# Global attention with separate score and maxima rings: the weighting issued once per step, behind both pairs of scores

## The chip, the cores and the metric

The kernel runs on one core of a Trainium2 chip. The metric is the device time of one execution in microseconds (us). TensorE (PE in the profile) multiplies matrices into PSUM, VectorE (DVE) and ScalarE (ACT) read PSUM, GpSimd (POOL) does small work on SBUF, SyncE (SP) mostly issues DMAs.

## The reference

A causal global attention and a local attention network read the same normalised input, and the output joins them. Only the global attention is touched by the change:

```python
scores = jnp.einsum('bhqd,bhkd->bhqk', q, k) / jnp.sqrt(jnp.asarray(D, x.dtype))
...
scores = jnp.where(causal[None, None], scores, -jnp.inf)
weights = jax.nn.softmax(scores, axis=-1)
out = jnp.einsum('bhqk,bhkd->bhqd', weights, v)
```

There are 16 heads of 16 numbers each and 4096 tokens. After it come the output projection, two layers of windowed attention and MLP, and a gate.

## The kernel before, in words

`global_attention` works on groups of four heads (4 groups, g) and blocks of 512 queries (8 blocks, j), 32 blocks in all; groups 0 and 2 run j upwards, groups 1 and 3 downwards. A block has one **step** for each tile of 128 keys that its queries may see, 4(j+1) of them, so 576 steps in all. The last four steps of a block are **diagonal**: the keys lie in the block's own range, the operands shrink to 512, 384, 256 and 128 queries, and a mask is added by a further matmul. The other 448 steps are **full**: 112 in each group.

A step has, for each of its four heads, a score matmul (128 keys by up to 512 queries, L585; its mask L592), an exponential on ScalarE (L485) that writes `probs`, and a weighting matmul (L606) that adds values times probabilities into the one bank `ps_o`. Heads go in two pairs, so a step has two **half-steps** (`hp` 0 and 1). In this text S0 to S3 are the four score matmuls of a step, E0 to E3 its exponentials.

The scores of the heads go through three PSUM banks, `ps_s` (SR = 3), in turn: score number n waits until exponential number n - 3 has been read out. So S3 of a step waits for E0 of the same step, and S2 for E3 of the step before.

The subtraction of the maximum is inside the score matmul, as extra rows of `qst`, so the row maxima of a block must be known before it starts. They come from a second pass of score matmuls, the **maxima**: a unit is two matmuls of up to 512 keys (L557, for the block's own keys a mask, L561), which VectorE reduces in one instruction (L509). Units have two PSUM slots of their own, `ps_m` (MR = 2); unit n waits for the reduction of unit n - 2. `pace` writes out in which half-step each unit is issued: mostly one, in group 0 every fourth half-step two, and a block's last unit about six half-steps before the block starts. When the last unit of a block is reduced, VectorE and GpSimd prepare the maxima, TensorE **turns** them (L567), VectorE copies them (L522) and SP issues their loads into `qst`; the block's first score waits for these.

ScalarE also copies `ps_o` out at the end of a block (`take_sums`, L474), behind the four exponentials of the next block's first step, and issues the loads of a later group's keys and values during the eight steps behind each of two group starts (L401 to L403).

TensorE takes its instructions in the order in which the block at the end of `global_attention` issues them. `weigh(s, half)` issues four matmuls, one for each head, over half of the queries (256 of 512 in a full step); each is two MATMUL records in the trace, so a half is "x8". The order before, for steps s and s+1:

```text
weigh(s, 0)   score(s+1, 1)   unit(s)   weigh(s, 1)   score(s+2, 0)   unit(s)   weigh(s+1, 0) ...
```

Of the kernel before, what the change touches and what calls it, by code (L numbers as in the profile page):

```python
# [17 lines left out]
C = 512  # L18
# [7 lines left out]
GH = 4  # L26
# [6 lines left out]
VW = 32  # L33
# [290 lines left out]
def global_attention(nc, k_parts, q_parts, v_aug, o_raw, ident, ones, nulls, identb, mask_k, mask_q):  # L324
# [5 lines left out]
    with ExitStack() as ctx:  # L330
        def sb(name, shape, dt=F32):
            return ctx.enter_context(nc.sbuf_tensor(name, shape, dt))
# [4 lines left out]
        QR, MR, SR, PR = 8, 2, 3, 3  # L337
        kst = [sb(f"kst{i}", [P, PAIRS, S], F32R) for i in range(2)]
        qst = [sb(f"qst{i}", [P, PAIRS, C], F32R) for i in range(QR)]
        vst = [sb(f"vst{i}", [P, NT, GH * VW]) for i in range(2)]  # L340
        probs = sb("probs", [P, PR, GH, C])
# [12 lines left out]
        ps_o = ctx.enter_context(nc.psum_tensor("ps_o", [P, C], F32))  # L354
# [14 lines left out]
        exp_done = sem("g_exp_done")  # L369
        pv_done = sem("g_pv_done")  # L370
        o_done = sem("g_o_done")
# [7 lines left out]
        NSTEP = len(steps)  # L379
        last_step = {st[0]: s for s, st in enumerate(steps)}  # L380
# [8 lines left out]
        def q_slot(b):  # L389
            return b % QR  # L390

        def q_use(b):
            return b // QR + 1
# [3 lines left out]
        def load_k(eng, g, j):  # L397
            cols = slice(j * C, (j + 1) * C)
            kh = k_parts[g * GH:(g + 1) * GH, :, :, cols].rearrange("(p x) t d n -> x (t d) p n", x=2)
            for x in range(2):  # L400
                eng.dma_start(kst[g % 2][ROWS * x:ROWS * x + 2 * D, :, cols].bitcast(F32), kh[x]).then_inc(k_in[g % 2][j], 16)  # L401
                eng.dma_start(kst[g % 2][ROWS * x + 2 * D:ROWS * x + KQ, :, cols].bitcast(F32), kh[x, 0:D]).then_inc(k_in[g % 2][j], 16)
            eng.dma_start(vst[g % 2][:, j * TPC:(j + 1) * TPC, :], v_aug[g, :, j * TPC:(j + 1) * TPC, :]  # L403
                          ).then_inc(k_in[g % 2][j], 16)
# [62 lines left out]
        @block.scalar  # L467
        def _(act):
            def take_sums(b):

                act.wait_ge(pv_done, 2 * last_step[b] + 2)
                if b >= 2:
                    act.wait_ge(o_out[b % 2], 16 * (b // 2))
                act.activation(o_sb[:, b % 2, :], ps_o[:, :], ACT.Copy).then_inc(o_done, 1)  # L474

            queue = []
            for s, (b, g, j, i) in enumerate(steps):
                off = max(0, i - TPC * j) * P

                if s >= PR:  # L480
                    act.wait_ge(pv_done, 2 * (s - PR) + 2)
                for h in range(GH):
                    n = GH * s + h
                    act.wait_ge(scored, n + 1)
                    act.activation(probs[:, s % PR, h, off:C], sslots[n % SR][:, off:C], ACT.Exp, scale=float(D) ** -0.5  # L485
                                   ).then_inc(exp_done, 1)
                if i == 0 and b > 0:
                    take_sums(b - 1)
                    if b % NC == 0 and b // NC + 1 < G:
                        queue = [(b // NC + 1, jj) for jj in range(NC)]  # L490
                elif queue:
                    load_k(act, *queue.pop(0))
            take_sums(NB - 1)
# [30 lines left out]
        @block.tensor  # L524
        def _(pe):
            pe.wait_ge(const_in, 12 * 16)
            pe.wait_ge(o_zero, 1)
            seen_k = set()
            seen_q = set()

            def need_k(g, j):
                for jj in range(j + 1):
                    if (g, jj) not in seen_k:
                        seen_k.add((g, jj))
                        pe.wait_ge(k_in[g % 2][jj], 16 * 5 * (g // 2 + 1))

            def do(unit):
                b = unit[1]
                g, j = order[b]
                n = place[unit]  # L540
                slot = mslots[n % MR]
                if n >= MR:
                    old = stream[n - MR]
                    if old[0] == "max":
                        pe.wait_ge(max_read, max_at[old] + 1)
                    else:
                        pe.wait_ge(mrow_done, old[1] + 1)
                if unit[0] == "max":
                    _, _, a, hp, cc = unit
                    if b not in seen_q:  # L550
                        seen_q.add(b)
                        pe.wait_ge(q_in[q_slot(b)], 16 * 6 * q_use(b))
                    need_k(g, cc)
                    width = P * (a + 1) if cc == j else C
                    for x in range(2):
                        rows = slice(ROWS * x, ROWS * x + ROWS)
                        last = pe.matmul(slot[:, x, 0:width], qst[q_slot(b)][rows, hp, a * P:(a + 1) * P],  # L557
                                         kst[g % 2][rows, hp, cc * C:cc * C + width], start=True, stop=True)
                    if cc == j:
                        for x in range(2):  # L560
                            last = pe.matmul(slot[:, x, a * P:width], id_b[:, :], mq_sb[:, :], start=False, stop=True,  # L561
                                             skip_group_check=True)
                    last.then_inc(max_scored, 1)
                else:
                    pe.wait_ge(split_done, b + 1)
                    for a in range(TPC):
                        last = pe.matmul(slot[0:GH * NPART, 0, a * P:(a + 1) * P],  # L567
                                         msplit[:, b % 2, a * GH:(a + 1) * GH, :].rearrange("p h t -> p (h t)").bitcast(F32),
                                         id_f[:, :], start=True, stop=True)
                    last.then_inc(turned, 1)  # L570

            def score(s, hp):
                b, g, j, i = steps[s]
                off = max(0, i - TPC * j) * P
                if i == 0 and hp == 0:

                    pe.wait_ge(m_in[q_slot(b)], 16 * GH * q_use(b))
                    need_k(g, j)
                diagonal = i >= TPC * j
                for x in range(2):  # L580
                    n = GH * s + 2 * hp + x
                    if n >= SR:
                        pe.wait_ge(exp_done, n - SR + 1)
                    rows = slice(ROWS * x, ROWS * x + ROWS)
                    last = pe.matmul(sslots[n % SR][:, off:C], kst[g % 2][rows, hp, i * P:(i + 1) * P],  # L585
                                     qst[q_slot(b)][rows, hp, off:C], start=True, stop=True)
                    if not diagonal:
                        last.then_inc(scored, 1)
                if diagonal:
                    for x in range(2):  # L590
                        n = GH * s + 2 * hp + x
                        pe.matmul(sslots[n % SR][:, off:off + P], id_b[:, :], mk_sb[:, :], start=False, stop=True,  # L592
                                  skip_group_check=True).then_inc(scored, 1)

            def weigh(s, half):
                b, g, j, i = steps[s]
                off = max(0, i - TPC * j) * P
                if half == 0:
                    if i == 0 and b > 0:

                        pe.wait_ge(o_done, b)
                    pe.wait_ge(exp_done, GH * s + GH)
                mid = (off + C) // 2
                lo, hi = ((off, mid), (mid, C))[half]
                for h in range(GH):
                    last = pe.matmul(ps_o[32 * h:32 * h + VW, lo:hi], vst[g % 2][:, i, h * VW:(h + 1) * VW],  # L606
                                     probs[:, s % PR, h, lo:hi], start=(i == 0 and half == 0), stop=(s == last_step[b]),
                                     tile_position=(0, 32 * h), skip_group_check=True)
                last.then_inc(pv_done, 1)

            for unit in first:
                do(unit)
            score(0, 0)
            score(0, 1)
            for t, (_, todo) in enumerate(plan):
                s, hp = t // 2, t % 2
                if hp:
                    weigh(s, 0)
                elif s >= 1:
                    weigh(s - 1, 1)  # L620
                if s + 1 < NSTEP:
                    score(s + 1, hp)
                for unit in todo:
                    do(unit)
            weigh(NSTEP - 1, 1)


def project_out(nc, y_rows, o_raw, w_o, b_o, bcast):
# [1006 lines left out]
```

## Time and profile before

| | before |
|---|---|
| median of 3 runs | 4113.04 us (4109.99 to 4122.79) |
| the profiled execution | 4123.71 us, its span 4121.9 us |
| PE busy in the span | 3442.6 us (84%) |
| DVE busy | 2534.4 us (61%) |
| ACT busy | 1695.8 us (41%) |
| mean granted TensorE clock | 0.921 of full |

The busy shares are averages over stages with different limits. The score matmuls of global attention run from 345 to 2037 us of the span. Timeline rows merge neighbouring instructions of a line: "x8" is eight instructions, the duration runs from the start of the first to the modelled end of the last. Ends of matmuls overlap the next instruction, so the cost of one to TensorE is read from its start to the start of what follows.

### The profile page before, as it was taken

The numbers are of one execution on the slowest core, as the hardware profiler recorded it, in microseconds if no ns is written. First come the engines' busy times: TensorE is split into PE (matmuls) and PEld (weight loads), VectorE is DVE, ScalarE is ACT, GpSimd is POOL, SyncE is SP. The second block draws the span as 40 slices with busy tenths as digits, with TensorE's granted clock in tenths as the row PEclk, the third lists the DMA queues.
The fourth block names the chain that finished last, engine by engine and source line by source line (L and its number), as shares of the span: only waits on it lengthen the run. The fifth ranks groups of instructions, "written<-read, shape, count | busy, mean of one in ns | idle before, by whom it ended". The sixth has DMA issues, their size and how long they took to land. (4 is left out here: it accounts for less than half of the span.)

```text
span 4121.9 us, 77619 instructions
## 1 busy us (share of the span) xinstructions
PE 3442.6 (84%) x32558; PEld 2063.7 (50%) x32684; DVE 2534.4 (61%) x3408; ACT 1695.8 (41%) x3089; POOL 669.0 (16%) x464
## 2 busy tenths in 40 slices
PE   5837999999999999999754899997697799996795
PEld 2412333333444333333333677775576677775675
DVE  4325887888777887766375555663454555553554
ACT  1203667677666777776400233231221233231221
POOL 4410000000000000000000433331132433331231
PEclk9956999999999999999777899998898999998898
DMA  4483000100021000000012000000000000000003
GB/s 161 144 143 79 17 9 17 43 26 10 17 61 47 17 17 9 4 4 7 29 66 74 22 17 17 14 15 2 26 0 28 22 17 17 17 12 16 12 0 122
DMA packets 83970, 141.78 MB, mean 34 GB/s; under 512 B 10992, under 2 KB 41840, under 8 KB 82688
## 3 DMA queue, kind: packets, MB, share of 16 engines
q1 hardware_dynamic: 77264, 126.84, 10.9%
q10 hardware_dynamic: 6400, 10.49, 1.1%
q8 instruction: 238, 3.90, 0.4%
q14 instruction: 68, 0.56, 0.0%
HBM read 94.23 MB, written 42.53 MB: 33 GB/s over the span
## 5 line engine op out<-in xcount | busy, mean ns | idle before, releaser
L509 DVE TENSOR_REDUCE mp<-ps_m 128x2 f32<-128x1024 f32 (+3 forms) x1152 | 1287.4, 1135 | 403.9 <-PE ps_m L557 280.9
L485 ACT ACTIVATE probs<-ps_s 128x512 f32<-128x512 f32 (+3 forms) x2304 | 1165.9, 560 | 633.6 <-PE ps_s L592 336.4
L606 PE MATMUL ps_o<-probs,vst 128*32 128x256 f32 (+3 forms) x9216 | 722.7, 386 | 3.4 <-ACT o_sb L474 2.4
L585 PE MATMUL ps_s<-qst,kst 64*128 64x512 f32 (+3 forms) x2304 | 597.6, 497 | 60.5 <-DMA qst<-mrow 52.3
L557 PE MATMUL ps_m<-kst,qst 64*128 64x512 f32 (+3 forms) x2304 | 488.2, 416 | 75.9 <-DMA qst<-null_rows 63.4
L585 PEld LDWEIGHTS ps_s<-qst,kst 64*128 64x128 f32 x2304 | 236.2, 190 | 525.1 <-ACT probs L485 431.6
L606 PEld LDWEIGHTS ps_o<-probs,vst 128*32 128x32 f32 x9216 | 187.5, 110 | 334.5 <-issue 218.0
L557 PEld LDWEIGHTS ps_m<-kst,qst 64*128 64x128 f32 x2304 | 230.5, 192 | 133.8 <-issue 70.1
L462 POOL TENSOR_TENSOR msplit<-negm,mzero 128x16 fp32r<-128x16 f32 x32 | 7.1, 221 | 1761.2 <-DVE negm L515 1761.2
L1178 DVE SCALAR_TENSOR_TENSOR a_t<-a_BP,a_sc,a_tab 128x256 f32<-128x256 f32 x384 | 167.0, 476 | 190.3 <-ACT a_sq L878 189.5
L857 ACT ACTIVATE a_PT<-a_SU 128x1024 f32<-128x1024 f32 (+1 forms) x128 | 122.4, 1009 | 342.6 <-PE a_SU L975 342.6
L833 POOL TENSOR_TENSOR a_rot<-a_t 128x512 f32<-128x512 f32 x128 | 163.1, 1274 | 530.5 <-DVE a_t L1178 530.5
L1346 ACT ACTIVATE m_gl<-m_bank_u,m_b 128x512 f32<-128x512 f32 x96 | 66.1, 688 | 345.6 <-PE m_bank_u L716 345.6
L1229 DVE RECIPROCAL a_rec<-a_B 128x256 f32<-128x256 f32 x64 | 112.5, 1758 | 127.4 <-PE a_B L1051 123.8
L839 POOL TENSOR_TENSOR a_rn<-a_ssc,a_half 128x32 f32<-128x32 f32 x32 | 174.0, 5438 | 93.8 <-DVE a_ssc L1223 93.8
L714 PE MATMUL m_bank_u<-m_hh,m_w1h 128*128 128x512 f32 x384 | 155.6, 405 | 29.1 <-DVE m_uf L1453 28.5
L1151 DVE TENSOR_REDUCE a_mx<-a_SU 128x4 f32<-128x1024 f32 (+1 forms) x128 | 148.6, 1203 | 50.7 <-PE a_SU L951 50.7
L1325 POOL TENSOR_TENSOR m_ul<-m_uf,m_uh 128x512 fp32r<-128x512 f32 x96 | 126.2, 1314 | 195.4 <-DVE m_uh L1459 195.4
L878 ACT ACTIVATE a_sq<-a_BP 128x512 f32<-128x512 f32 x128 | 76.5, 598 | 191.4 <-PE a_BP L716 191.4
L715 PE MATMUL m_bank_u<-m_hl,m_w1h 128*128 128x512 f32 x384 | 153.1, 399 | 0.0
L716 PE MATMUL m_bank_u<-m_hh,m_w1l 128*128 128x512 f32 x384 | 152.9, 398 | 0.0
L714 PE MATMUL a_BP<-a_hTh,a_wqh 128*128 128x256 f32 x512 | 149.8, 293 | 1.6 <-DVE a_t L1178 1.5
(159 smaller groups left out, 5387.4 us busy)
## 6 DMA issues: line engine op xcount, KB each, us to landing
a_tab<-in_rope SPq DMA_DIRECT2D x32, 512.0 KB, 3.6
q_parts<-pparts SPq DMA_DIRECT2D x32, 256.0 KB
k_parts<-pparts SPq DMA_DIRECT2D x32, 256.0 KB
v_aug<-pvsb SPq DMA_DIRECT2D x32, 256.0 KB
qst<-q_parts SPq DMA_DIRECT2D x64, 128.0 KB, 2.8
o_raw<-o_sb SPq DMA_DIRECT2D x32, 256.0 KB, 2.1
oraw<-o_raw SPq DMA_DIRECT2D x8, 1024.0 KB, 5.0
X<-in_x SPq DMA_DIRECT2D x8, 512.0 KB, 9.4
```

Of the source, the lines that this page charges most:

```text
L485: act.activation(probs[:, s % PR, h, off:C], sslots[n % SR][:, off:C], ACT.Exp, scale=float(D) ** -0.5).then_inc(exp_done, 1)
L509: dve.tensor_reduce(mp[b % 2][:, h:h + 2, cc:cc + 1], slot[:, :, 0:width], AX.X, ALU.max).then_inc(max_read, 1)
L557: last = pe.matmul(slot[:, x, 0:width], qst[q_slot(b)][rows, hp, a * P:(a + 1) * P], kst[g % 2][rows, hp, cc * C:cc * C + width], start=Tr ...
L585: last = pe.matmul(sslots[n % SR][:, off:C], kst[g % 2][rows, hp, i * P:(i + 1) * P], qst[q_slot(b)][rows, hp, off:C], start=True, stop=True)
L606: last = pe.matmul(ps_o[32 * h:32 * h + VW, lo:hi], vst[g % 2][:, i, h * VW:(h + 1) * VW], probs[:, s % PR, h, lo:hi], start=(i == 0 and h ...
L714: pe.matmul(out, a_hi, b_hi, start=start, stop=False)
L715: pe.matmul(out, a_hi, b_lo, start=False, stop=False)
L716: return pe.matmul(out, a_lo, b_hi, start=False, stop=stop)
L833: pool.tensor_tensor(rot[:, g, :, :].rearrange("p a b -> p (a b)"), t[:, n % 2, 0, :, :].rearrange("p a b -> p (a b)"), t[:, n % 2, 1, :, ...
L839: pool.tensor_tensor(rn[:, :, :, :].rearrange("p a b c -> p (a b c)"), ssc[:, :, :, :].rearrange("p a b c -> p (a b c)"), half[:, :], ALU. ...
L1151: dve.tensor_reduce(mx[:, w % 2, 2 * b:2 * b + 2, :], SU[:, 2 * b:2 * b + 2, :].rearrange("p i (q c) -> p i q c", q=2)[:, :, :, lo:N2], AX ...
L1178: dve.scalar_tensor_tensor(out=dst, in0=src, scalar=s, in1=table, op0=ALU.mult, op1=ALU.mult).then_inc(rope_done, 1)
```

## The change

The weighting of a step is no longer split into halves of its queries. `weigh(s)` issues its four matmuls over the whole 512 columns (or 384, 256, 128 in diagonal steps), once per step. It stands behind both pairs of scores of the next step and their maxima. The semaphore `pv_done` counts once per step in place of twice, and the ScalarE waits on it are rewritten to match. The work of VectorE, GpSimd and SP, `pace`, and the rings stay as they are.

The order after:

```text
score(s+1, 0)   unit(s)   score(s+1, 1)   unit(s)   weigh(s)   score(s+2, 0) ...
```

```diff
-                act.wait_ge(pv_done, 2 * last_step[b] + 2)
+                act.wait_ge(pv_done, last_step[b] + 1)
...
-                    act.wait_ge(pv_done, 2 * (s - PR) + 2)
+                    act.wait_ge(pv_done, s - PR + 1)
...
-            def weigh(s, half):
+            def weigh(s):
...
-                if half == 0:
-                    if i == 0 and b > 0:
-
-                        pe.wait_ge(o_done, b)
-                    pe.wait_ge(exp_done, GH * s + GH)
-                mid = (off + C) // 2
-                lo, hi = ((off, mid), (mid, C))[half]
+                if i == 0 and b > 0:
+
+                    pe.wait_ge(o_done, b)
+                pe.wait_ge(exp_done, GH * s + GH)
                 for h in range(GH):
-                    last = pe.matmul(ps_o[32 * h:32 * h + VW, lo:hi], vst[g % 2][:, i, h * VW:(h + 1) * VW],
-                                     probs[:, s % PR, h, lo:hi], start=(i == 0 and half == 0), stop=(s == last_step[b]),
+                    last = pe.matmul(ps_o[32 * h:32 * h + VW, off:C], vst[g % 2][:, i, h * VW:(h + 1) * VW],
+                                     probs[:, s % PR, h, off:C], start=(i == 0), stop=(s == last_step[b]),
                                      tile_position=(0, 32 * h), skip_group_check=True)
...
                 s, hp = t // 2, t % 2
-                if hp:
-                    weigh(s, 0)
-                elif s >= 1:
-                    weigh(s - 1, 1)
                 if s + 1 < NSTEP:
                     score(s + 1, hp)
                 for unit in todo:
                     do(unit)
-            weigh(NSTEP - 1, 1)
+                if hp:
+                    weigh(s)
```


## Rows read from the trace of the kernel before

**Rows 1.** Windows: busy us of each engine (instructions), TensorE clock, DMA share, GB/s.

```profile
345.00:2037.00 1692.00, 1609.38 (x14998) 653.54 (x14998) 1287.45 (x1184) 1179.25 (x2336) 13.28 (x60) 0.95 0.07 20
618.17:687.46 69.29, 67.56 (x610) 26.46 (x611) 63.46 (x58) 52.27 (x97) 0.00 (x0) 0.95 0.04 13
1538.00:1605.00 67.00, 67.00 (x658) 25.43 (x654) 62.15 (x54) 57.99 (x107) 0.00 (x0) 1.00 0.03 9
1618.00:1626.00 8.00, 7.40 (x50) 2.72 (x50) 0.00 (x0) 5.13 (x10) 0.00 (x0) 0.50 0.32 95
```

**Rows 2.** Timeline of full steps: start us, us, engine, line, operation, count, idle before.

```profile
1550.48 0.50 PE L585 MATMUL ps_s<-qst,kst 64*128 64x512 f32 x2
...
1550.82 0.40 PE L557 MATMUL ps_m<-kst,qst 64*128 64x512 f32 x2
1551.08 2.26 ACT L485 ACTIVATE probs<-ps_s 128x512 f32<-128x512 f32 x4 [0.21 <-PE ps_s L585]
...
1551.15 0.64 PE L606 MATMUL ps_o<-probs,vst 128*32 128x256 f32 x8
...
1551.72 0.51 PE L585 MATMUL ps_s<-qst,kst 64*128 64x512 f32 x2
...
1552.96 0.50 PE L585 MATMUL ps_s<-qst,kst 64*128 64x512 f32 x2
```

**Rows 3.** Groups by line and shape, 345 to 2037 us: busy us, mean ns, idle before.

```profile
L509 DVE TENSOR_REDUCE mp<-ps_m 128x2 f32<-128x1024 f32 x945 | 1141.4, 1224 | 303.9 <-PE ps_m L557 278.6 <-PE ps_m L561 18.9
L485 ACT ACTIVATE probs<-ps_s 128x512 f32<-128x512 f32 x1920 | 1039.4, 596 | 451.7 <-PE ps_s L585 258.6 <-PE ps_s L592 158.9 <-PE ps_o L606 8.5
```

**Rows 4.** Timeline of the first full step of a block (previous block's weighting).

```profile
1338.55 0.32 PE L606 MATMUL ps_o<-probs,vst 128*32 128x64 f32 x8
...
1338.80 0.83 PE L585 MATMUL ps_s<-qst,kst 64*128 64x512 f32 x2
...
1340.41 0.63 ACT L474 ACTIVATE o_sb<-ps_o 128x512 f32<-128x512 f32 x1
...
1340.89 1.14 ACT L485 ACTIVATE probs<-ps_s 128x512 f32<-128x512 f32 x2
```

**Rows 5.** Timeline of diagonal steps.

```profile
1517.67 0.50 PE L585 MATMUL ps_s<-qst,kst 64*128 64x512 f32 x2
...
1518.10 0.28 PE L592 MATMUL ps_s<-mk_sb,id_b 128*128 128x128 bf16 x2
...
1518.32 0.50 PE L557 MATMUL ps_m<-kst,qst 64*128 64x512 f32 x2
1518.43 1.09 ACT L485 ACTIVATE probs<-ps_s 128x512 f32<-128x512 f32 x2 [0.38 <-PE ps_s L592]
...
1518.75 0.64 PE L606 MATMUL ps_o<-probs,vst 128*32 128x256 f32 x8
...
1525.33 0.53 PE L606 MATMUL ps_o<-probs,vst 128*32 128x192 f32 x8
...
1525.79 0.38 PE L585 MATMUL ps_s<-qst,kst 64*128 64x256 f32 x2
```

**Rows 6.** Timeline of steps whose key and value loads ScalarE issues.

```profile
806.28 0.49 PE L585 MATMUL ps_s<-qst,kst 64*128 64x512 f32 x1 [0.64 <-ACT probs L485]
...
806.94 0.64 PE L606 MATMUL ps_o<-probs,vst 128*32 128x256 f32 x8
...
807.51 0.50 PE L585 MATMUL ps_s<-qst,kst 64*128 64x512 f32 x2
...
808.74 0.45 ACTq L403 DMA_DIRECT2D vst<-v_aug  x1
```

**Rows 7.** Timeline: first score of block 6 (group 0), and that of its first diagonal step.

```profile
618.17 0.80 PE L585 MATMUL ps_s<-qst,kst 64*128 64x512 f32 x2 [2.24 <-DMA qst<-mrow]
...
687.46 0.49 PE L585 MATMUL ps_s<-qst,kst 64*128 64x512 f32 x2
```

**Rows 8.** Timeline: first score of a later block, and what it waits for.

```profile
1618.47 0.80 PE L585 MATMUL ps_s<-qst,kst 64*128 64x512 f32 x2 [2.24 <-DMA qst<-mrow]
```

## The prediction, before the changed kernel was timed

> **What bounds the kernel now.** I read the windows view first, for the stretch of the 576 steps and for a stretch inside one block [rows 1]. Over the whole stretch of 1692 us the granted clock is 0.95, and TensorE is busy for 1609 us. Between 1538 and 1605 us, in full steps, it is busy for 67.00 of 67.00 us at full clock, VectorE for 62 and ScalarE for 58. So TensorE looks like the bound, and anything that shortens its work looks like a gain. A busy TensorE includes modelled ends, so the timeline of these steps [rows 2] has to say what releases each instruction.
>
> In the timeline a pair of scores starts at 1550.48, its unit of maxima 0.34 us later, a half weighting 0.33 after that (1551.15), and the next pair of scores 0.57 after that (1551.72). The sum is 1.24 us for a half-step and 2.48 for a step (the next S0 starts at 1552.96). Beside it runs a second path of the same length: S0 at 1550.48, E0 at 1551.08 (0.60 later), 0.596 us for an exponential of this shape [rows 3], and S3, which waits for the bank that E0 frees, in the pair at 1551.72, 0.04 after E0's end. That is 1.24 us too. So between S0 and S3 TensorE has exactly as much work (scores, unit, half a weighting) as the ring of three banks makes it wait. The third limit is VectorE: a unit of full width takes 1.224 us [rows 3], two in a step 2.45.
>
> **The change part by part.**
>
> *One weighting for two halves.* A half of 256 columns costs TensorE 0.57 us, start to start [rows 2]; one of 192 takes 0.46 [rows 5] and one of 64 takes 0.25 [rows 4]. That is 0.107 us for each 64 columns on top of about 0.14. By this line 512 columns cost 1.00 us. The old pair cost 1.14, so TensorE's own work shrinks by 0.14 us a step. No instruction of 512 columns stands in the trace. Its bounds are 0.86 (the slope alone, no fixed part) and 1.14 (nothing saved); I take 1.00, since the rows lie on a line.
>
> *The move.* Half a weighting stood between S0 and S3; now nothing of it does, and the whole weighting stands behind S3. S3 still waits for E0, so it starts 1.24 us after S0, but the work in between is only scores and unit, 0.34 + 0.33 = 0.67 us. The cover of 0.57 us is gone, and TensorE waits that long in each step. Behind the waiting S3 stand in TensorE's queue a unit and the whole weighting, and the next S0 waits for both. ScalarE waits for that S0. From a late S3 to the weighting takes 0.66 us, 806.28 to 806.94 [rows 6], where the row shows S3 held for ScalarE. The new step: 1.24 + 0.66 + 1.00 = 2.90 us against 2.48, +0.42. ScalarE is no limit in it: E3 comes at least three exponentials behind E0, and the weighting needs the E3 of the step before, which ended long ago. `probs` has three slots and the weighting is late by less than one step, so the new `pv_done` counts make nobody wait.
>
> The Trainium skill, TensorE: Matmul & The Clock Gate (Part 3, The mechanism), says that weight loads may be pulled ahead but that matmuls start and end in program order. It speaks against the change: by it the weighting can't slip into the wait in front of S3. The trace agrees where S3 is late, since nothing of the weighting runs before 806.94 [rows 6]. With matmuls free to pass, the sum would be the one of the first rival below.
>
> *How many steps pay.* The counts come from the order that `pace` writes out. Groups 1 to 3 have 336 full steps.
> - 276 have two units, no turn and nothing special: a third have a narrow unit, whose mask is half of the time hidden in the new wait, so I take +0.41. That is 113 us.
> - 14 have a turn in their second half-step. TensorE waits there for VectorE and GpSimd, the first half weighting was hidden in that wait, and the whole one now follows it: +0.42 each, 6 us.
> - 21, early in the blocks of group 3, have no unit or one. The cover lost is the same: +0.45, 9 us (bounds 6 and 12).
> - 14 are the first of a block with the narrow weighting of the step before, 0.25 in place of 1.14 us; they are bound by the ring already: +0.1, 1 us.
> - 11 carry loads of keys and values on ScalarE's queue, five at about 0.45 us [rows 6]. These hold E0 back in either order, and the sum of them and four exponentials stays: 0.
>
> *Group 0* has 112 full steps, half of them with three units. In block 6, 24 of them take 69.29 us, 2.89 a step [rows 7], with VectorE busy for 63.46 [rows 1]. Here VectorE is near its limit (2.64 a step). After: 2.90 with two units, about 3.15 with three (0.25 is VectorE's row divided over its wait and TensorE's second unit; bounds 0.15 and 0.5), mean 3.02. +0.13 times 112: 15 us, bounds 0 and 35.
>
> *Diagonal steps* (128). In the first one the ring is longer: S0 at 1517.67, E0 at 1518.43, exponential 0.60, 0.04: 1.40 us. Then 0.43 + 0.22 + 0.43 to the weighting and 1.00 for it [rows 5]: 3.48, against twice 1.65 before (1517.67 to 1518.75, and 0.57): +0.18. The second pays about +0.07, the third nothing, the fourth gains 0.1, because exponentials and weighting shrink. In some 13 blocks the last two are free: the next block's first score waits 2.24 us for its maxima anyway [rows 8], and that time runs from the last unit. Together +5 us.
>
> *Block turnover.* `take_sums` stands on ScalarE ahead of the second step's E0; its copy starts at 1340.41 and the exponential 0.48 later [rows 4]. In the new order this E0 releases S3 with no weighting ahead of it: 0.2 us in 31 places, 6 us, bounds 0 and 18.
>
> Stages outside the global attention aren't touched.
>
> **Sum.** 113 + 6 + 9 + 1 + 15 + 5 + 6 = 155 us, made on the profiled execution: 4123.71 + 155 = 4279. The median of the runs lies 10.7 us below that execution, so the forecast for the median is 4113 + 155 = 4268 us, 3.8% slower.
>
> **Rivals.**
>
> 1. *TensorE's work is what counts (faster).* In favour: it was busy 67.00 of 67.00 us. Then the 0.14 us saved in each step is a gain, but VectorE caps it: a step of two full units can't fall below 2.45, so 0.03 us in some 276 steps (8), up to 0.1 where a unit is narrow (9), 0.14 in the diagonal ones (18): 35 us, 4078. It decides if S3 could start within 0.82 us of S0 (2.48 less 0.66 and 1.00). Against it: S0 to E0 0.60 and E0's 0.596 are both in the rows, and together exceed 0.82. In the Trainium skill, TensorEngine Tiling (Array Packing), Key Properties, changing the tiling mode drains TensorE; the new order changes mode less often. By that alone, an estimate of 0.14 us in 576 steps is 82 us, 4031. The fixed 0.14 us of a weighting is in line with such a drain; that it bounds the step is what I dispute.
>
> 2. *The clock falls as well.* The new wait leaves TensorE idle for a fifth of a step. Behind a stall, in steps without units, the granted clock is 0.50, the lower of its levels, 1.2 GHz (the last row of [rows 1]). At it 1.66 of the 2.90 us double, so a step takes 4.6. If a tenth more of some 1850 us ran so, about 70 us are added: 4338. Against: a diagonal step gives TensorE less to do in more time, and its scores of 512 columns keep the 0.50 us that they have at full clock [rows 2, 5].
>
> 3. *Slower by half only.* VectorE or the waits for the maxima absorb more (over the stretch a step takes 1692 / 576 = 2.94 us, not 2.48, so other waits exist), or S0 to S3 falls to 1.05 us when nothing of the weighting runs in it. 0.2 us a step in 400 steps: 4193.
>
> 4. *The order is no bound at all* and nothing moves: 4113.
>
> **How the numbers follow.** The main case has 0.82, the falling clock 0.07, the half case 0.05, the faster one 0.04, no change 0.02. The main case's own bounds: a weighting at 1.14 adds 59 us over some 420 steps; group 0, turnover and steps without units at their ends move it by −24 or +35; +0.36 in place of 0.41 takes 14 off. Range 4205 to 4335. About 0.3% of the time, 12 us, is what a measurement of this kernel can tell from no change: faster 0.04, within it 0.03, slower 0.93.
>
> **What would show it.** In a full step after: S0, S3 1.24 us later and released by ScalarE, a wait of about 0.55 us in front of it, the eight weighting records starting 0.66 behind S3, the next S0 1.00 behind them, and 2.90 us from S0 to S0. VectorE should be idle about 0.45 us a step, ScalarE 0.9. The busy time of the weighting should fall, its count from 9216 to 4608. The forecast is wrong if S3 starts with S2, if 512 columns cost other than 1.00, or if the clock of the stretch leaves 0.95.

## The result, and the profile after

The changed kernel is slower: 4316.27 us in the median against 4117.91. The forecast was 3.8% slower, with 4268 us; the range of 4205 to 4335 holds the time. The profiled execution of that result was an outlier of 7805.65 us, in which most kinds of matmul, in every stage, took 1.4 to 2.4 times as long: the ratio is therefore that of the fast runs alone, 1.0467 (95% interval 1.0430 to 1.0504), and all rows of the changed kernel below are from `again`, a second profile of the same code (4321.15 us, ratio 1.0513, 1.0488 to 1.0537).

Its page, over a span of 4312.4 us: the busy times, and the groups by line (busy us, mean ns, idle before and its main releaser).

```profile
PE 3558.3 (83%) x28076; PEld 2066.4 (48%) x28076; DVE 2537.8 (59%) x3408; ACT 1654.0 (38%) x3089; POOL 669.5 (16%) x464
...
L509 DVE TENSOR_REDUCE mp<-ps_m 128x2 f32<-128x1024 f32 (+3 forms) x1152 | 1292.6, 1136 | 573.3 <-PE ps_m L557 388.3
...
L585 PE MATMUL ps_s<-qst,kst 64*128 64x512 f32 (+3 forms) x2304 | 791.2, 483 | 142.8 <-ACT probs L485 101.1
...
L603 PE MATMUL ps_o<-probs,vst 128*32 128x512 f32 (+2 forms) x4608 | 614.0, 604 | 0.0
```

The weighting is at L603 now, with 4608 records in place of 9216, as it should be. VectorE and ScalarE do the same work as before (1152 reductions, 2304 exponentials), but VectorE waits 573 us in front of its reductions where it waited 404, and the scores wait 101 us for ScalarE.

The timeline of a full step after, which answers to [rows 2]:

```profile
1492.30 0.50 PE L585 MATMUL ps_s<-qst,kst 64*128 64x512 f32 x2
...
1492.64 0.40 PE L557 MATMUL ps_m<-kst,qst 64*128 64x512 f32 x2
...
1492.88 0.39 PE L585 MATMUL ps_s<-qst,kst 64*128 64x512 f32 x1
1492.90 2.06 ACT L485 ACTIVATE probs<-ps_s 128x512 f32<-128x512 f32 x4 [0.83 <-PE ps_s L585]
1493.08 2.46 DVE L509 TENSOR_REDUCE mp<-ps_m 128x2 f32<-128x1024 f32 x2 [0.44 <-PE ps_m L557]
...
1493.55 0.50 PE L585 MATMUL ps_s<-qst,kst 64*128 64x512 f32 x1 [0.28 <-ACT probs L485]
...
1493.55 0.73 PE L557 MATMUL ps_m<-kst,qst 64*128 64x512 f32 x2
...
1494.21 1.06 PE L603 MATMUL ps_o<-probs,vst 128*32 128x512 f32 x8
...
1495.20 0.50 PE L585 MATMUL ps_s<-qst,kst 64*128 64x512 f32 x2
```

S0 starts at 1492.30 and E0 at 1492.90. S2 goes out alone at 1492.88, since its bank has long been free. S3 has to wait until 1493.55, 1.25 us behind S0, and its row names ScalarE as the releaser; E0 (0.60 long) ended at 1493.50. The weighting follows 0.66 later, at 1494.21, takes 0.99 us to the next S0 at 1495.20, and the step has 2.90 us. The four lengths (1.25, 0.66, 0.99 and 2.90) were forecast to a hundredth. The idle time in front of S3 was not: its row has 0.28 us, where about 0.55 was forecast, because S2, which now runs alone, fills a part of the gap. VectorE's idle time is 0.44 us, as forecast.

Now the whole stretch (from its start to the last score) and one step with a turn in it; columns as in [rows 1].

```profile
345.00:2214.00 1869.00, 1698.37 (x10363) 645.82 (x10362) 1292.92 (x1184) 1134.79 (x2329) 13.34 (x60) 0.94 0.06 18
1137.12:1144.17 7.05, 5.58 (x30) 2.17 (x26) 3.66 (x5) 2.06 (x4) 0.45 (x2) 0.76 0.00 0
```

The mean granted clock of the stretch is 0.94, about as before (0.95), but the step with the turn, 5.16 us before, now takes 7.05 us and its granted clock is 0.76. More on that below.

From the start times of all S0 in the two profiles, the steps can be summed by kind (us; the last column is the term of the forecast):

```text
steps of the global attention           count   before    after    more   forecast
groups 1-3, full, two units               277    703.8    818.4    +115    +113
full, with a turn                          14     72.6     88.4     +16      +6
full, no unit or one (group 3)             21     65.8     78.4     +13      +9
first full step of a block                 14     33.1     33.4       0      +1
full, with loads on ScalarE                10     34.6     37.9      +3       0
group 0, full                             112    325.9    362.1     +36     +15
diagonal                                  125    444.5    444.2       0      +5
(block turnover, in the rows above)                                           +6
all, with the first two                   575   1688.3   1871.3    +183    +155
```

The span of these two profiles grew by 190.5 us, so nearly all of it lies where the change is.

### The profile page after: what moved, and what is told of

Same layout as the page of the kernel before. It is cut to its first block and busy times, and to the rows that moved or that the text cites. A ratio compares the mean times of both kernels' runs of the same rounds, so it can differ in the third digit from the quotient of the medians.

```text
span 7803.8 us, 68529 instructions
## 1 busy us (share of the span) xinstructions
PE 7350.3 (94%) x28076; PEld 3651.6 (47%) x28076; DVE 2533.4 (32%) x3408; ACT 1711.9 (22%) x3089; POOL 664.1 (9%) x464
## 5 line engine op out<-in xcount | busy, mean ns | idle before, releaser
L603 PE MATMUL ps_o<-probs,vst 128*32 128x512 f32 (+2 forms) x4608 | 1311.6, 1258 | 0.0
L557 PE MATMUL ps_m<-kst,qst 64*128 64x512 f32 (+3 forms) x2304 | 964.9, 741 | 66.8 <-DMA qst<-null_rows 59.9
L585 PE MATMUL ps_s<-qst,kst 64*128 64x512 f32 (+3 forms) x2304 | 927.5, 692 | 29.5 <-DMA qst<-mrow 25.7
L557 PEld LDWEIGHTS ps_m<-kst,qst 64*128 64x128 f32 x2304 | 421.7, 310 | 154.9 <-issue 91.7
L930 PE MATMUL a_SU<-a_mask,a_idb 128*128 128x512 bf16 x512 | 329.0, 802 | 11.7 <-DVE a_mx L1145 5.0
L1045 PE MATMUL a_BP<-a_PT,a_V 128*32 128x256 f32 (+1 forms) x3008 | 315.9, 636 | 6.7 <-ACT a_negm L859 3.6
L969 PE MATMUL a_SU<-a_QK 32*128 32x256 f32 (+1 forms) x2368 | 317.4, 738 | 0.0
L228 PE MATMUL pps_p<-pxT,pw 128*128 128x512 f32 x256 | 307.0, 1439 | 9.5 <-ACT pxT L200 9.5
L945 PE MATMUL a_SU<-a_QK 32*128 32x256 f32 (+1 forms) x2368 | 311.7, 725 | 0.0
L709 PE MATMUL a_BP<-a_hTl,a_wqh 128*128 128x256 f32 x512 | 274.6, 536 | 0.0
L710 PE MATMUL a_BP<-a_hTh,a_wql 128*128 128x256 f32 x512 | 274.3, 536 | 0.0
```

Of the source, the lines that this page charges most:

```text
L603: last = pe.matmul(ps_o[32 * h:32 * h + VW, off:C], vst[g % 2][:, i, h * VW:(h + 1) * VW], probs[:, s % PR, h, off:C], start=(i == 0), sto ...
L709: pe.matmul(out, a_hi, b_lo, start=False, stop=False)
L710: return pe.matmul(out, a_lo, b_hi, start=False, stop=stop)
L930: pe.matmul(SU[:, i, :], idb_sb[:, :], mask[:, :], start=True, stop=False, skip_group_check=True)
L945: last = pe.matmul(SU[:, i, q * N2 + off:q * N2 + off + n], QK[rows, 4 * q + d, a:a + P], QK[rows, 4 * q + 2 + d, at:at + n], start=False, ...
L969: last = pe.matmul(SU[:, i, q * N2 + off:q * N2 + off + n], QK[rows, 4 * q + 2 + d, a:a + P], QK[rows, 4 * q + d, at:at + n], start=False, ...
```

## The experiments

All start from the changed kernel's file or from the one before. Ratios are against the kernel before, run on the same chip.

```text
run             median us   ratio to before (95%)
again             4321.15   1.0513 (1.0488 to 1.0537)
halves_late       4323.80   1.0508 (1.0478 to 1.0538)
whole_between     4253.23   1.0349 (1.0324 to 1.0375)
units_first       4222.28   1.0267 (1.0242 to 1.0291)
bank3_old         4623.21   1.1217 (1.1161 to 1.1274)
bank3_new         4332.65   1.0538 (1.0505 to 1.0572)
bank4_old         4666.78   not settled (4513.91 to 4905.22)
bank4_new         4049.38   0.9860 (0.9827 to 0.9894)
short_new         4217.32   1.0265 (1.0237 to 1.0293)
short_old         4110.64   0.9996 (0.9982 to 1.0010)
hybrid            4111.99   0.9995 (0.9983 to 1.0007)
```

### again

No edit.

> The changed kernel once more, for a profile at an ordinary clock. Ring theory (S3 waits for E0 of its own step with nothing to cover it): a full step takes 2.90 us, S3 starts 1.24 us after S0 released by ScalarE, the weighting of 512 columns takes 1.00 us, the time is 4300 to 4325 us. Width theory (the instruction of 512 columns is itself what costs, the new place is free): S3 starts with S2, 0.67 us after S0, and the weighting takes 1.57 us or more. Clock theory: steps of 2.5 us where the clock is full, but a mean granted clock of the stretch well under 0.95.

As the ring theory has it: 2.90 us, S3 released by ScalarE, the weighting 0.99. The width theory is out, since 512 columns cost less than twice 256. The clock theory is out as the main cause: 264 of the 277 steps with two units ran wholly at full clock, and their median is 2.90 us.

### halves_late

```diff
                 if hp:
-                    weigh(s)
+                    weigh(s, 0)
+                    weigh(s, 1)
```

> The order of the changed kernel, but the weighting again in two halves, both behind the second scores. Ring theory: the wait in front of S3 stays and the weighting costs 1.14 in place of 1.00, so a full step takes 3.04 us and the time is some 75 us above the changed kernel, about 4385. Width theory: the halves cost what they did before, so the time goes back to about 4118.

The timeline of a step (the 16 records are both halves):

```profile
1550.53 0.50 PE L585 MATMUL ps_s<-qst,kst 64*128 64x512 f32 x2
...
1551.77 0.49 PE L585 MATMUL ps_s<-qst,kst 64*128 64x512 f32 x1 [0.28 <-ACT probs L485]
...
1552.43 1.07 PE L605 MATMUL ps_o<-probs,vst 128*32 128x256 f32 x16
...
1553.43 0.50 PE L585 MATMUL ps_s<-qst,kst 64*128 64x512 f32 x2
```

The time is that of `again`, not 75 us more. The place alone makes the whole loss. And the two halves take 1.00 us side by side, 1552.43 to 1553.43, no more than the whole. So the 0.14 us saved isn't a fixed part of an instruction: it is paid where the weighting stands next to something else, and is saved as well by putting halves together. In the Trainium skill, TensorEngine Tiling (Array Packing), Key Properties, a change of tiling mode drains TensorE. The trace agrees in so far as 0.14 us is paid once for each run of weightings, not once for each group of four; no run here tells a drain from another cost of going over to the weighting.

### whole_between

```diff
                 s, hp = t // 2, t % 2
+                if hp:
+                    weigh(s)
                 if s + 1 < NSTEP:
                     score(s + 1, hp)
                 for unit in todo:
                     do(unit)
-                if hp:
-                    weigh(s)
```

> The whole weighting, but between the two pairs of scores (where the first half stood before), none of it behind the second pair. Ring theory: S3 finds its bank free, but the cover is now missing on the other side: the next step's S1 waits for E2, 1.18 us after S2; a full step takes 1.67 + 1.18 = 2.85 us, so the time is only some 20 us under the changed kernel, about 4290. Rival (only the place in front of S3 matters): 2.34 to 2.48 us a step, the time at or under 4118. Width theory: the same as the changed kernel, 4310.

The timeline from S2 and S3 (1550.77) over the next S0 (1551.33) and its S1 (1551.95) to the next S2:

```profile
1550.77 0.50 PE L585 MATMUL ps_s<-qst,kst 64*128 64x512 f32 x2
...
1551.33 0.39 PE L585 MATMUL ps_s<-qst,kst 64*128 64x512 f32 x1
...
1551.95 0.49 PE L585 MATMUL ps_s<-qst,kst 64*128 64x512 f32 x1 [0.22 <-ACT probs L485]
...
1552.61 1.06 PE L603 MATMUL ps_o<-probs,vst 128*32 128x512 f32 x8
...
1553.60 0.50 PE L585 MATMUL ps_s<-qst,kst 64*128 64x512 f32 x2
```

The wait has moved to the other side of the step. S1 waits for ScalarE, 1.18 us behind S2 as expected, and the step takes 2.83 us. So it isn't the place in front of S3 that matters but that one of the two gaps has no cover. The time fell by 68 us, not 20. By the sums over S0 starts the stretch is 42 us shorter: the full steps with two units give 15, the steps with a turn 32 (below), block starts 11 and group 0 7, and the other diagonal steps take 23 back. The rest lies outside the stretch, which takes 2416 to 2441 us in the profiles of these kernels for code that is the same; so a single profile is good to some 20 us for a total, and to a hundredth for the median of a kind of step.

### units_first

```diff
-                for unit in todo:
-                    do(unit)
+                if hp == 0:
+                    for unit in todo + plan[t + 1][1]:
+                        do(unit)
                 if hp:
                     weigh(s)
```

> The changed kernel with both half-steps' maxima units issued between the two pairs of scores, so that other work covers the wait in front of S3. Ring theory: S0 to S3 stays at 1.24 us, but S3 to the next S0 falls from 1.66 to 1.34 us, so a full step takes 2.58 us; 0.32 us in 336 steps and about 0.1 in those of group 0, where VectorE is near its limit, is some 110 us less than the changed kernel, about 4200, still above 4118. Width theory and clock theory: no difference from the changed kernel, 4310.

A step, from S0 to the next:

```profile
1551.45 0.50 PE L585 MATMUL ps_s<-qst,kst 64*128 64x512 f32 x2
...
1552.33 0.87 PE L585 MATMUL ps_s<-qst,kst 64*128 64x512 f32 x2
...
1553.13 1.06 PE L603 MATMUL ps_o<-probs,vst 128*32 128x512 f32 x8
...
1554.12 0.50 PE L585 MATMUL ps_s<-qst,kst 64*128 64x512 f32 x2
```

A unit in the gap makes a step of 2.67 us, against 2.58 expected and 2.90 before the edit: cover of any kind helps. What is off is the weighting's start, 1.68 us behind S0, since scores followed directly by a weighting take 0.43 us, not 0.33. The time fell by 99 us of the 110 expected.

### bank3_old, bank3_new, bank4_old, bank4_new

The maxima hold four PSUM banks, the scores three and `ps_o` one. Here a fourth for the scores is taken from the maxima. Each unit computes the even head of its pair only, in one bank, and VectorE reads it twice; this leaves out half of the maxima matmuls.

```diff
-        QR, MR, SR, PR = 8, 2, 3, 3
+        QR, MR, SR, PR = 8, 2, 4, 3      # bank4; 3 in bank3
...
-        mslots = [ctx.enter_context(nc.psum_tensor(f"ps_m{i}", [P, 2, C], F32)) for i in range(MR)]
+        mslots = [ctx.enter_context(nc.psum_tensor(f"ps_m{i}", [P, C], F32)) for i in range(MR)]
...
-                    for x in range(2):
+                    for x in range(1):
                         rows = slice(ROWS * x, ROWS * x + ROWS)
-                        last = pe.matmul(slot[:, x, 0:width],
+                        last = pe.matmul(slot[:, 0:width],
```

> A control with a bank set free. The kernel before, but a maxima unit computes the even head of its pair only, in a slot of one bank, and VectorE reads that bank twice, so that the odd head is scaled by the even head's maximum (half of the maxima matmuls are left out). VectorE's time and the three score banks stay. Old order: about as before, 4090 to 4125 us, 2.48 us a full step.

> The same halved maxima in the changed kernel's order, still three score banks. Ring theory: the wait in front of S3 doesn't depend on the maxima, 2.90 us a full step, some 190 us above its partner in the old order, about 4300.

> Halved maxima, old order, the free bank given to the scores (four in turn). Ring theory: TensorE's 2.48 and VectorE's 2.45 us remain, so at most 15 us less than with three banks.

> Halved maxima, the changed kernel's order, four score banks. Ring theory: S3 now waits for E3 of the step before, which has ended, so the wait is gone, TensorE needs 2.34 us a step and VectorE 2.45: the loss of 190 us turns into a gain over the old order with four banks, 0 to 40 us, about 4080. If the loss came from the weighting's width, its late place or the clock alone, it stays near 4300.

Two successive S0 in `bank4_new`, with S2 and S3, VectorE's reductions and the weighting between them:

```profile
1376.01 0.50 PE L586 MATMUL ps_s<-qst,kst 64*128 64x512 f32 x2
...
1376.35 0.62 PE L586 MATMUL ps_s<-qst,kst 64*128 64x512 f32 x2
...
1376.78 5.83 DVE L509 TENSOR_REDUCE mp<-ps_m 128x2 f32<-128x1024 f32 x5 [0.28 <-PE ps_m L558]
...
1377.14 1.07 PE L604 MATMUL ps_o<-probs,vst 128*32 128x512 f32 x8
...
1378.13 0.50 PE L586 MATMUL ps_s<-qst,kst 64*128 64x512 f32 x2
```

S2 and S3 go out together, 0.34 us behind S0, without a wait. The weighting starts 1.13 behind S0 and the step takes 2.12 us here, though others take up to 2.5. Over all full steps at full clock the medians are

```text
score banks          3      4
old order         2.45   2.45
new order         2.67   2.36
```

So a fourth bank takes 0.31 us off the new order and nothing off the old one, and the change turns from a loss of 0.22 us a step into a gain of 0.1. From S0 to S3 the new order takes 1.24 us in the median with three banks and 0.59 with four (steps with two units in groups 1 to 3). Two sizes were off. With one matmul in a unit the new order has 2.67, not 2.90, since that matmul runs beside the late S3, and the weighting follows S3 by 0.43 us, not 0.66, as in this step of `bank3_new`:

```profile
1506.37 0.49 PE L586 MATMUL ps_s<-qst,kst 64*128 64x512 f32 x1 [0.28 <-ACT probs L485]
...
1506.38 0.49 PE L558 MATMUL ps_m<-kst,qst 64*128 64x512 f32 x1
...
1506.80 1.06 PE L604 MATMUL ps_o<-probs,vst 128*32 128x512 f32 x8
```

And VectorE caps later than at 2.45. A reduction of full width still lasts 1.22 us, but of two that follow each other without a wait the second starts 1.14 us (median) behind the first: five take 5.83 us in the row at 1376.78, not 6.1. Two in a step are 2.28 us, and where both units have full width the median step is 2.25 us. In the kernel before such pairs stand as close (1.13 us at the least).

The times of the old-order pair were far from expected, and the windows of the same 1605 us say why: the first is `bank3_old`, then `bank3_new`, `bank4_old` and `bank4_new`. The last three columns are the granted clock, the DMA share and GB/s.

```profile
345.00:1950.00 1605.00, 1581.15 (x9499) 583.73 (x9499) 962.92 (x879) 819.01 (x1618) 9.30 (x42) 0.61 0.06 18
```

```profile
345.00:1950.00 1605.00, 1470.51 (x7594) 538.97 (x7594) 1125.25 (x1041) 962.17 (x1965) 10.66 (x48) 0.85 0.07 19
```

```profile
345.00:1950.00 1605.00, 1567.27 (x10497) 590.46 (x10492) 1057.83 (x963) 906.39 (x1790) 10.19 (x46) 0.70 0.07 20
```

```profile
345.00:1950.00 1605.00, 1495.68 (x8977) 593.91 (x8976) 1249.66 (x1184) 1123.00 (x2321) 13.28 (x60) 0.93 0.08 21
```

With half of the maxima matmuls left out, the old order ran at a granted clock of 0.61 and 0.70, for long stretches at the lower level of 1.2 GHz, although TensorE was busy for 98% of the time. That is where 4623 and 4667 us come from. The new orders leave out the same matmuls and ran at 0.85 and 0.93, so the work left out is not the whole cause, and no run here shows the rest of it. The four are a comparison of steps at full clock, not of total times. `bank4_new` alone, with a clock of 0.93, can be set beside the kernel before: it is 1.4% faster (4049 us, where about 4080 was expected), but it leaves out half of the maxima matmuls, so it doesn't show that the change would pay in a kernel that computes all of them.

### short_new and short_old

The exponential of each full-width step's first head takes 256 of its 512 columns, the rest of its probabilities are zero. TensorE's work is untouched.

```diff
+                    end = C // 2 if h == 0 and off == 0 else C
-                    act.activation(probs[:, s % PR, h, off:C], sslots[n % SR][:, off:C], ACT.Exp,
+                    act.activation(probs[:, s % PR, h, off:end], sslots[n % SR][:, off:end], ACT.Exp,
```

> The changed kernel, with the exponential of each full-width step's first head over 256 of its 512 columns (the other half of its probabilities stays zero: work left out on ScalarE alone, TensorE's work is all there). Ring theory: E0 lasts 0.38 in place of 0.60 us (the 256-column exponential before), S3 starts that much earlier, a full step falls from 2.90 to 2.69 us, and the time by 0.21 us in some 430 steps, 90 us, to about 4230. If TensorE's work, the weighting's shape or the clock alone made the loss, nothing changes: 4320.

> The same shorter first exponential in the kernel before. There half a weighting covers the whole of the ring's 1.24 us, so a full step stays at 2.47 us and the time within 10 us of before.

First `short_new`, then `short_old`; S0, the exponentials, what follows, and the next S0:

```profile
1551.72 0.50 PE L587 MATMUL ps_s<-qst,kst 64*128 64x512 f32 x2
...
1552.32 1.85 ACT L486 ACTIVATE probs<-ps_s 128x256 f32<-128x256 f32 x4 [0.83 <-PE ps_s L587]
...
1552.75 0.73 PE L559 MATMUL ps_m<-kst,qst 64*128 64x512 f32 x2
...
1553.41 1.06 PE L605 MATMUL ps_o<-probs,vst 128*32 128x512 f32 x8
...
1554.41 0.50 PE L587 MATMUL ps_s<-qst,kst 64*128 64x512 f32 x2
```

```profile
1550.49 0.50 PE L587 MATMUL ps_s<-qst,kst 64*128 64x512 f32 x2
...
1551.09 0.87 ACT L486 ACTIVATE probs<-ps_s 128x256 f32<-128x256 f32 x2 [0.21 <-PE ps_s L587]
...
1551.73 0.50 PE L587 MATMUL ps_s<-qst,kst 64*128 64x512 f32 x2
...
1552.96 0.50 PE L587 MATMUL ps_s<-qst,kst 64*128 64x512 f32 x2
```

In the new order the unit that follows S3 starts at 1552.75, 1.03 us behind S0 in place of 1.25, and the step falls to 2.69 us; the time falls by 104 us (90 expected). In the old order the step stays at 2.47 and the time too. The same 0.22 us of ScalarE's time is worth a hundred microseconds in one order and nothing in the other. This is the most direct evidence that E0 lies on the path after the change.

### hybrid

Before's order, with `weigh` whole where the width is 256 (behind the scores) or 128 (between them).

```diff
+                return {2: "late", 3: "between"}.get(i - TPC * j, "halves")
...
+                if hp and place_of(s) != "late":
+                    weigh(s, 0 if place_of(s) == "halves" else None)
+                elif not hp and s >= 1 and place_of(s - 1) == "halves":
+                    weigh(s - 1, 1)
...
+                if hp and place_of(s) == "late":
+                    weigh(s)
```

> The kernel before, halves and order, except for the narrow weightings: that of a block's third diagonal step (256 columns) whole behind the second scores, as in the changed kernel, and that of its fourth (128 columns) whole between the two pairs of scores. By the rows of the earlier runs a step with the first falls from 2.59 to 2.39 us where nothing else holds it (20 places), one with the second from 2.15 to 1.83 (21 places): some 11 us less than before, about 4100, at the edge of what can be told. If the whole weighting costs wherever it stands, it is slower than before.

The first full step of a block took 2.15 us before where nothing else held it, and takes 1.73 now (from 963.89 to 965.62 in one of them); 1.83 was expected. The step with the 256 columns fell from 2.52 to 2.39, likewise where nothing else held it. Summed over the profile, the first steps of the blocks gain 13.5 us and the other kind 1.7. The steps right behind the first ones take 10.0 us back and all others 4.7, so the stretch is 1687.9 us against 1688.3, and 12 runs can't tell the kernel from the one before. Why it comes back was not tried. No kernel that computes everything beat the one before.

## Why the prediction was right, and where its sizes were off

**The main step held.** S3 waits for E0 of its own step; half a weighting covered that wait; moved behind S3 it covers nothing. The full step was forecast at 2.90 us and is 2.90, and 277 such steps cost 115 us against 113. `short_new` and `short_old` show that E0 is what counts, `bank4_new` beside `bank3_new` that the number of banks is, `units_first` that cover of another kind restores part of it. The sum is less sure than its step: 155 us were forecast and 183 measured in the stretch, with terms that missed on both sides and in part made up for each other, as told below. The counts in the kernel are 277 and 10, where the prediction has 276 and 11.

**The weighting's cost held** (1.00 forecast, 0.99 measured), **its reason was half right**. The prediction took the fixed 0.14 us as a part of each weighting; it goes with a run of weightings, so `halves_late` costs no more than the whole.

**The rivals.** TensorE's work as the bound fails: its weighting did get shorter (0.99 us in place of 1.14) and the step longer. The cap of 2.45 us that VectorE was given there, and as the third limit, is too high too: the steps of `bank4_new` with two units of full width take 2.25 us in the median. "Half only" and "no bound" fail with the 2.90. The falling clock isn't the main cause, but it has a share, next.

**Steps with a turn** missed as much as group 0 below: +16 in place of +6 in full steps, and +11 in 16 diagonal ones where nothing was counted. In `again` (below), TensorE waits 1.47 us between the scores and the turn (L567), and the granted clock falls to its lower level inside the step (the second fence is a window, with columns as in [rows 1]).

```profile
1140.32 1.86 PE L567 MATMUL ps_m<-id_f,msplit 128*8 128x128 f32 x8 [1.47 <-POOL msplit L464]
...
1142.84 1.40 PE L603 MATMUL ps_o<-probs,vst 128*32 128x512 f32 x8
...
1144.17 0.50 PE L585 MATMUL ps_s<-qst,kst 64*128 64x512 f32 x2
```

```profile
1140.32:1142.84 2.52, 2.52 (x10) 1.17 (x11) 0.62 (x1) 0.00 (x0) 0.00 (x0) 0.50 0.00 0
```

The turn's eight records take 1.86 us where the same in `whole_between` take 1.03, and the weighting, at first at the lower level, 1.33 where it takes 0.99. Six of the 14 full steps with a turn kept full clock, and these take 5.63 us, 0.44 more than before: that is the term as forecast. The others lost the rest to the clock. The same step in `whole_between`, where the weighting stands between the two pairs of scores and the wait for the turn is 0.82 us:

```profile
1122.93:1128.04 5.11, 4.06 (x28) 1.71 (x27) 2.88 (x4) 3.11 (x6) 0.45 (x2) 1.00 0.00 0
```

It keeps full clock and takes 5.11 us. All 14 there keep full clock, and so did all 14 before. Over the stretch the time at the lower clock rose from 156 to 230 us between the two profiles. So the forecast, which gave the clock 0.07 as a case of its own, should have had it as a small term of the main case, at the places where the wait for a turn grows.

**Group 0** cost +36 in place of +15. A step with three units:

```profile
593.11 0.50 PE L585 MATMUL ps_s<-qst,kst 64*128 64x512 f32 x2
...
594.36 1.31 PE L557 MATMUL ps_m<-kst,qst 64*128 64x512 f32 x4
595.16 0.19 PEld L557 LDWEIGHTS ps_m<-kst,qst 64*128 64x128 f32 x2 [0.52 <-DVE mp L509]
...
595.60 1.07 PE L603 MATMUL ps_o<-probs,vst 128*32 128x512 f32 x8
...
596.59 0.50 PE L585 MATMUL ps_s<-qst,kst 64*128 64x512 f32 x2
```

S3 and the two units behind it now stand close together. The second unit waits for VectorE (0.52 in its row) until the slot that it read from 593.88 is free, and the step takes 3.48 us; 3.15 was forecast. The second unit costs 0.58, beyond my bounds of 0.15 and 0.50. In the median the steps with three units went from 3.06 to 3.48 us, and those with two from 2.52 to 2.90, which is where the forecast had them, so the miss is the second unit's. The mistake was to take VectorE as near its limit and so as a cover; with the units bunched it waits first (0.70 us in front of 593.88) and is late afterwards.

**Diagonal steps** came out at 0 against +5, with +11 at the turns and −18 in the third and fourth steps, far more than the 2 or 3 that I gave them. Loads on ScalarE cost +3.

**The block turnover** was put at +6 on top of the steps' own loss, and this failed. The second steps of blocks (12 full ones with two units in groups 1 to 3) take 3.09 us in the median, 0.19 more than the usual 2.90, as forecast. But they took 2.85 before, already 0.37 more than 2.48, which the prediction left out, so they lost 0.24 us and not 0.6.

## What to carry to other kernels

A busy TensorE isn't yet the bound: compare the sum of its work between two dependent instructions with the length of the ring between them. Here the two were 1.24 and 1.24 us, so the half weighting moved out of that gap (0.57 us) was paid in full, less the 0.14 us that the merge saved. By the same reckoning work saved inside the gap would be worth nothing, which no run here shows. Before merging instructions that stand on two sides of a dependency, ask what the far one was covering; if the saving is in neighbourhood rather than size, it comes with the move and not with the merge. With a fourth bank the same edit shortened the step instead (2.36 us against 2.45, with half of the maxima matmuls left out), so order and ring depth have to be tuned together.

## What the runs showed of the hardware that was not expected

- Two half weightings side by side (16 records) cost 1.00 us, one whole 0.99, two apart 1.14.
- A kernel with less work for TensorE can be 12% slower through its clock: with half of the maxima matmuls left out, the old order ran its stretch at a granted clock of 0.61 against 0.95, and at 4623 us against 4112, while its steps at full clock were as short as before (2.45 us). The new order with the same matmuls left out had 0.85. Why they differ is open.
- A maxima unit of one matmul ran beside a late S3 (`bank3_new`) and made the step 0.23 us shorter than a unit of two.
- VectorE's full-width reductions last 1.22 us each, but without a wait between them they start 1.13 to 1.14 us apart, so their mean duration is too high a price for a row of them.
